# A two-layer graph network: the node block between the layers with its own-part product issued one step ahead and its turn two steps ahead

## The chip, the cores and the metric

The kernel runs on one core of a Trainium2 chip, on real inputs, as one program. The metric is the time of the whole program on the device in microseconds, the median of several runs; lower is better.

## What is computed

The reference applies two graph layers to 6250 nodes of 128 features with 200000 edges `src -> dst`. Ahead of each layer stands a layer norm (no gain, no bias) with a ReLU, and each layer's result is added to its input. Cut to what matters here:

```python
h = relu(layernorm(x))
sums = segment_sum(h[dst], src) + 2 * h;  reduced = sums / (count + 1)
x = x + relu(concat([reduced, h]) @ kernel + bias)            # layer 0
h = relu(layernorm(x))                                        # between the layers
q, k, v = h[src] @ Wq.T + bq, h[dst] @ Wk.T + bk, h[dst] @ Wv.T + bv
att = exp(clip(q.k per head / 4, -10, 10));  out = segment_sum(att / att_sum[src] * v, src)
x = x + layernorm(out + h) * gamma + beta                     # layer 1
```

## The kernel before

The kernel sorts the edges into 49 bins of 128 nodes and then runs layer 0's gathers and segment sums (L526, L1003 to L1005, L767), a **node block between the layers** (L1230 to L1458), layer 1's gathers, attention and sums (L1491 to L1649), and a last node block. The blocks follow one another; within a block each engine has its own program, and semaphores join them.

The block between the layers works in 13 steps of four bins (`NODE_STEPS` = 13, `NT` = 4; the last step has one bin). In step k:

- ScalarE's `first(k)` writes `hs`, the ReLU of the first layer norm (L1393, four instructions), waits for TensorE to have turned it, and copies the turned tiles from PSUM bank 7 to `hT0` (L1399).
- TensorE's `own(k)` turns the four tiles of `hs` (L1358), waits for that copy (`s_e0`), and multiplies: a bias product (L1368) and a product with the lower half of the layer's weights (L1369) for each tile, into bank 6. The reduced half's product is already summed in `acc`.
- VectorE's `update(k)` adds both parts (L1235), adds to `xs` with a ReLU (L1240), and computes the statistics of the second layer norm (L1244 to L1249). ScalarE's `root(k)` takes the root (L1403), VectorE's `scale(k)` makes scale and shift (L1254, L1256), and ScalarE's `normal(k)` writes the second `hs` (L1408).
- TensorE's `turn(k)` turns these tiles (L1340), ScalarE's `copy_h(k)` copies them (L1417), and TensorE's `project(k)` multiplies them with the three weight matrices, 384 columns for each tile (L1349).
- VectorE's `add_bias(k)` writes `qkv` (L1268); SP's queue writes keys and values to DRAM (L1452); ScalarE's `high` (L1421) and `middle` (L1425) and GpSimd's `take_rest` and `take_low` (L1319, L1324) split the queries into three bf16 parts. GpSimd's `plus_beta` (L1314) and `clear` (L1307) prepare layer 1.

The order on every engine is written out by hand: a loop over k calls each stage with a fixed lag. Every engine runs its own instructions in that order. Bank 7 holds one step's turned tiles, bank 6 one step's products, and `hT0` two steps.

Of the kernel before, what the change touches and what calls it, by code (L numbers as in the profile page):

```python
# [82 lines left out]
NODE_STEPS = -(-BINS // NT)  # L83
# [13 lines left out]
def build(nc, x, src, dst, k0, b0, wq, bq, wk, bk, wv, bv, gamma, beta, out):  # L97
# [70 lines left out]
    with ExitStack() as phase:  # L168
# [8 lines left out]
        with nc.Block() as block:  # L177
            c_pool = Count(sem("s_const"))

            @block.sync  # L180
            def _(sp):
                sp.wait_ge(s_pad, 2)
                with nc.allow_non_contiguous_dma("the last edges, one to a partition"):
                    for a, t in ((src, src_i), (dst, dst_e)):
                        sp.dma_start(t[:, 0:FULL], a[0:FULL * P].rearrange("(p c) -> p c", c=FULL))\
                          .then_inc(s_edge, 16)
                        sp.dma_start(t[0:TAIL, FULL:FULL + 1],
                                     a[FULL * P:N_EDGES].rearrange("(p c) -> p c", c=1)).then_inc(s_edge, 16)
                sp.wait_ge(s_xpad, 1)
                head = (BINS - 1) * P  # L190
                sp.dma_start(xs0[:, 0:BINS - 1, :],
                             x[0:head, :].rearrange("(n p) f -> p n f", p=P)).then_inc(s_x, 16)
                sp.dma_start(xs0[0:LAST_NODES, BINS - 1, :], x[head:N_NODES, :]).then_inc(s_x, 16)
# [54 lines left out]
    with ExitStack() as phase:  # L248
# [153 lines left out]
        with nc.Block() as block:  # L402
            @block.sync
            def _(sp):
# [25 lines left out]
                def numbers(row, top):  # L430
                    _, regs = nc.values_load_multi_w_load_instructions(
                        row, engines=[mybir.EngineType.SP], min_val=0, max_val=top,
                        skip_runtime_bounds_check_because="counts of at most N_EDGES edges, beside a bin's start")
                    return regs
# [107 lines left out]
            def _(v):  # L542
# [210 lines left out]
                def add(k, g):  # L753
                    i0 = g * G
                    u = group0[k] + g
                    if i0 % REGS == 0:
                        v.wait_ge(s_rows, k + 1)
                        n = min(REGS, cuts0(k) - i0)
                        _, regs[0] = nc.values_load_multi_w_load_instructions(
                            bin0_row[0:1, k % 2, i0:i0 + n], engines=[mybir.EngineType.DVE], min_val=0,  # L760
                            max_val=BINS - 1, skip_runtime_bounds_check_because="a count of 48 comparisons")
                    v.wait_ge(s_m0, u + 1)
                    for i in range(members(k, g)):
                        if u or i:
                            v.wait_ge(s_a0, added[u] + i)
                        o = acc[:, bass.ds(regs[0][(i0 + i) % REGS], 1), 0:W0].rearrange("p a b -> p (a b)")
                        v.tensor_tensor(out=o, in0=o, in1=bank[5 + u % 3][:, i * W0:(i + 1) * W0], op=ALU.add)\  # L767
                         .then_inc(s_a0, 1)
# [418 lines left out]
    with ExitStack() as phase:  # L1187
# [37 lines left out]
        with nc.Block() as block:  # L1225
# [107 lines left out]
            @block.tensor  # L1333
            def _(t):
                def turn(k):
                    t.wait_ge(s_h1, k + 1)
                    if k >= 2:
                        t.wait_ge(s_e1, k - 1)
                    for i in range(nt(k)):
                        ins = t.transpose(bank[k % 2][:, i * P:(i + 1) * P], hs[:, k * NT + i, :], ident[:, :])  # L1340
                    ins.then_inc(s_t1, 1)

                def project(k):
                    t.wait_ge(s_e1, k + 1)
                    for i in range(nt(k)):
                        n = k * NT + i
                        if n >= 4:
                            t.wait_ge(s_qkv, n - 3)
                        t.matmul(bank[2 + n % 4][:, 0:3 * D], hT1[:, k % 2, i * P:(i + 1) * P],  # L1349
                                 wT[:, :, :].rearrange("p a b -> p (a b)"), start=True, stop=True)\  # L1350
                         .then_inc(s_mm1, 1)

                def own(k):
                    t.wait_ge(s_h0, k + 1)
                    if k:
                        t.wait_ge(s_e0, k)
                    for i in range(nt(k)):
                        ins = t.transpose(bank[7][:, i * P:(i + 1) * P], hs[:, k * NT + i, :], ident[:, :])  # L1358
                    ins.then_inc(s_t0, 1)
                    t.wait_ge(s_e0, k + 1)  # L1360
                    if k:
                        t.wait_ge(s_x1, k)
                    else:
                        t.wait_ge(s_wl2, 16 * 6)
                        t.wait_ge(s_one, 1)
                    for i in range(nt(k)):
                        o = bank[6][:, i * D:(i + 1) * D]
                        t.matmul(o, one_r[:, :], b0_r[:, :], start=True, stop=False)  # L1368
                        ins = t.matmul(o, hT0[:, k % 2, i * P:(i + 1) * P], k0_s[:, 1, :], start=False, stop=True)  # L1369
                    ins.then_inc(s_own, 1)  # L1370

                for i, (a, b) in enumerate(quads):
                    t.wait_ge(s_nat[i], 16 * (b - a))
                    for j in range(a, b):
                        ins = t.transpose(bank[2 + i][:, (j - a) * P:(j - a + 1) * P], nat[:, j, :], ident[:, :])
                    ins.then_inc(s_natT, 1)
                for k in range(NODE_STEPS + 3):
                    if k < NODE_STEPS:
                        own(k)
                    if 0 <= k - 2 < NODE_STEPS:  # L1380
                        turn(k - 2)
                    if k >= 3:
                        project(k - 3)

            @block.scalar
            def _(a):
                def first(k):
                    m = nt(k)
                    for i, (p, q) in enumerate(x_pieces):
                        if k == p:  # L1390
                            a.wait_ge(s_x2[i], 16 if q < NODE_STEPS else 32)
                    for n in range(k * NT, k * NT + m):
                        ins = a.activation(hs[:, n, :], xs[:, n, :], ACT.Relu, scale=rstd[:, n:n + 1],  # L1393
                                           bias=nbias[:, n:n + 1])
                    ins.then_inc(s_h0, 1)
                    a.wait_ge(s_t0, k + 1)
                    if k >= 2:
                        a.wait_ge(s_own, k - 1)
                    a.activation(hT0[:, k % 2, 0:m * P], bank[7][:, 0:m * P], ACT.Copy).then_inc(s_e0, 1)  # L1399

                def root(k):
                    a.wait_ge(s_var1, k + 1)
                    a.activation(rstd[:, cut(k)], rstd[:, cut(k)], ACT.Sqrt).then_inc(s_root1, 1)  # L1403

                def normal(k):
                    a.wait_ge(s_ln1, k + 1)
                    for n in range(k * NT, k * NT + nt(k)):
                        ins = a.activation(hs[:, n, :], xs[:, n, :], ACT.Relu, scale=rstd[:, n:n + 1],  # L1408
                                           bias=nbias[:, n:n + 1])
                    ins.then_inc(s_h1, 1)  # L1410

                def copy_h(k):
                    m = nt(k) * P
                    a.wait_ge(s_t1, k + 1)
                    if k >= 2:
                        a.wait_ge(s_mm1, (k - 1) * NT)
                    a.activation(hT1[:, k % 2, 0:m], bank[k % 2][:, 0:m], ACT.Copy).then_inc(s_e1, 1)  # L1417

                def high(k):
                    a.wait_ge(s_qkv, k * NT + nt(k))  # L1420
                    a.activation(q3[:, cut(k), 0:D], qkv[:, k % 4, 0:nt(k), 0:D], ACT.Copy).then_inc(s_qhi, 1)  # L1421

                def middle(k):
                    a.wait_ge(s_left, k + 1)
                    a.activation(q3[:, cut(k), D:2 * D], left[:, k % 2, 0:nt(k), :], ACT.Copy)\  # L1425
                     .then_inc(s_qmid, 1)

                for k in range(NODE_STEPS + 5):
                    for lag, stage in ((0, first), (1, root), (2, normal), (2, copy_h), (4, high), (5, middle)):
                        if 0 <= k - lag < NODE_STEPS:  # L1430
                            stage(k - lag)

# [342 lines left out]
```

## Time and profile before

| | |
|---|---|
| timed runs, us | 6179.91 median of 3 (6173.57 to 6182.65) |
| profiled execution, us | 6125.97, of which the span of instructions is 6124.2 |
| busy in the whole span, us | TensorE 3137.7, VectorE 3081.1, ScalarE 1860.1, GpSimd 3189.0 |
| mean granted clock of TensorE | 0.614 |
| the block between the layers | 3188 to 3336 us of the span |

The granted clock is given as a share of 2.4 GHz; 0.50 is 1.2 GHz and 1.00 is 2.4 GHz, and a value between them is a stretch in which both occurred. In the rows below PE is TensorE, PEld its weight loads, DVE VectorE, ACT ScalarE, POOL GpSimd. Times are from the start of the span. In order-of-time rows, adjacent instructions of one line are merged ("x4"), and the idle time in brackets is that before the first of them.

### The profile page before, as it was taken

The page shows a single profiled execution, that of the slowest core. Times are in us where ns is not written, and L with a number is a line of the kernel's source. Part 1 is how long each engine was busy: PE and PEld are TensorE (multiplying, and loading weights), DVE is VectorE, ACT ScalarE, POOL GpSimd, SP SyncE. Part 2 cuts the span into 40 slices and gives each one's busy share as a digit, 9 for nine tenths or more (in the row PEclk, how much of TensorE's full clock was granted, in tenths as well). Part 3 has the DMA queues.
Part 4 walks back from the last instruction along what each step waited for, and adds up shares of the span by engine and source line. Part 5 has one row for each costly group of instructions (what it writes and reads, how often), then busy time and mean ns, then how long its engine had stood idle before and what let it go on. Part 6 is the DMA issues. An engine that isn't in the chain of part 4 may idle for free. (4 is left out here: it accounts for less than half of the span.)

```text
span 6124.2 us, 86465 instructions
## 1 busy us (share of the span) xinstructions
PE 3137.7 (51%) x21028; PEld 2407.9 (39%) x21028; DVE 3081.1 (50%) x8514; ACT 1860.1 (30%) x5489; POOL 3189.0 (52%) x3338
## 2 busy tenths in 40 slices
PE   4445445444454354354356555555555555555553
PEld 3223334333233233243234444444444444444442
DVE  6435445455454364354234555555555555555557
ACT  3232433333233333333344222222222222222222
POOL 3363463553543644644634555555555555555554
PEclk8556555556565565565557666666666666666665
DMA  2231231322322322322321222222222222222223
GB/s 78 55 83 47 70 77 49 76 69 51 82 56 56 86 53 60 81 60 64 89 54 63 78 79 79 79 79 79 78 78 79 79 79 79 79 79 79 79 78 58
DMA packets 205061, 436.91 MB, mean 71 GB/s; under 512 B 67172, under 2 KB 114781, under 8 KB 204606
## 3 DMA queue, kind: packets, MB, share of 16 engines
q0 software_dynamic: 153968, 371.50, 23.0%
q1 hardware_dynamic: 49934, 59.56, 3.6%
q8 instruction: 219, 3.59, 0.2%
q14 instruction: 236, 1.93, 0.1%
q10 hardware_dynamic: 704, 0.33, 0.0%
HBM read 415.27 MB, written 55.69 MB: 77 GB/s over the span
## 5 line engine op out<-in xcount | busy, mean ns | idle before, releaser
L526 POOL DMA_INDIRECT got<-hk_table,dst x1563 | 1524.6, 975 | 1487.1 <-PE bank L1005 837.0
L1491 POOL DMA_INDIRECT kv<-kv_table,dst_i x1611 | 1527.1, 948 | 1177.1 <-DVE wv_s L1533 732.5
L767 DVE TENSOR_TENSOR acc<-acc,bank 128x129 f32 x2187 | 634.5, 290 | 1300.2 <-remote 670.8
L1003 PE MATMUL bank<-got,oh 128*128 x2187 | 614.7, 283 | 1294.6 <-DVE acc L767 774.0
L1551 DVE TENSOR_TENSOR acc<-acc,bank 128x136 f32 x1611 | 469.8, 292 | 1232.7 <-remote 822.0
L1003 PEld LDWEIGHTS bank<-got,oh 128*128 128x128 bf16 x2187 | 239.5, 109 | 1495.4 <-issue 1449.3
L1106 ACT ACTIVATE oh<-away 128x384 bf16<-128x384 bf16 x733 | 383.1, 523 | 1392.1 <-remote 803.4
L1622 PE MATMUL bank<-identb,oh 128*128 128x128 bf16 x1611 | 250.1, 286 | 1072.5 <-DVE oh L1504 830.6
L1649 PE MATMUL bank<-wv_s,oh_f 128*128 128x136 f32 x3222 | 782.0, 404 | 3.6 <-DVE wv_s L1533 3.5
L1638 PE MATMUL bank<-q,ohT 128*128 x4833 | 670.4, 276 | 117.4 <-issue 65.1
L1100 ACT ACTIVATE away<-iota,negx 128x128 bf16<-128x128 f32 x2187 | 707.2, 386 | 0.0
L1590 ACT ACTIVATE ohT<-bank 128x384 bf16<-128x384 bf16 x537 | 263.8, 491 | 1444.6 <-remote 1364.8
L1649 PEld LDWEIGHTS bank<-wv_s,oh_f 128*128 128x128 f32 x3222 | 654.4, 287 | 8.9 <-DVE wv_s L1533 4.5
L1005 PE MATMUL bank<-got,oh 128*128 x2187 | 613.1, 282 | 79.9 <-issue 79.6
L1004 PE MATMUL bank<-got,oh 128*128 x2187 | 613.7, 282 | 73.2 <-issue 71.5
L1622 PEld LDWEIGHTS bank<-identb,oh 128*128 128x128 bf16 x1611 | 151.3, 126 | 1167.6 <-DVE oh L1504 883.0
L1638 PEld LDWEIGHTS bank<-q,ohT 128*128 128x128 bf16 x4833 | 496.1, 112 | 283.1 <-issue 193.2
L960 PE MATMUL bank<-oh_t,val 128*128 128x128 f16 x3128 | 350.0, 286 | 73.2 <-issue 48.5
L960 PEld LDWEIGHTS bank<-oh_t,val 128*128 128x128 f16 x3128 | 301.0, 143 | 80.2 <-issue 51.9
L1533 DVE TENSOR_TENSOR wv_s<-kv,bank 128x384 f32<-128x384 f32 x537 | 294.0, 548 | 23.8 <-ACT bank L1601 22.5
L1504 DVE TENSOR_TENSOR oh<-bank,r 128x384 bf16<-128x384 f32 x537 | 295.5, 551 | 7.2 <-ACT bank L1578 7.2
L1512 DVE TENSOR_TENSOR prod<-bank,kv 128x384 f32<-128x384 f32 x537 | 294.4, 548 | 5.8 <-DMA kv<-kv_table,dst_i 3.2
(223 smaller groups left out, 3394.6 us busy)
## 6 DMA issues: line engine op xcount, KB each, us to landing
slots_by_bin<-sorted_chunk SPq DMA_DIRECT2D x637, 61.0 KB
kv<-kv_table,dst_i POOLq DMA_INDIRECT x1611
got<-hk_table,dst POOLq DMA_INDIRECT x1563
kv_table<-qkv SPq DMA_DIRECT2D x12, 512.0 KB, 2.9
hk_table<-hk POOLq DMA_DIRECT2D x6, 772.0 KB, 5.5
out<-o SPq DMA_DIRECT2D x12, 256.0 KB
xs<-in_x SPq DMA_DIRECT2D x3, 768.0 KB, 11.4
sorted_chunk<-vT SPq DMA_DIRECT2D x13, 64.0 KB
```

The source lines that it names most:

```text
L526: g.indirect_dma_start(out=got[:, (tile0[k] + t) % RING0, :], out_offset=None, in_=hk_d, in_offset=bass.IndirectOffsetOnAxis(dst0[:, k % 2 ...
L767: v.tensor_tensor(out=o, in0=o, in1=bank[5 + u % 3][:, i * W0:(i + 1) * W0], op=ALU.add)\
L960: ins = t.matmul(bank[4][:, l * P:(l + 1) * P], val[:, q % 2, l * BLK:(l + 1) * BLK, :, j].rearrange("p w j -> p (w j)"), oh_t[:, q % 2, j ...
L1003: t.matmul(o, w, row(2 * D, 3 * D + 1), start=True, stop=False)
L1004: t.matmul(o[:, 0:D], w, row(D, 2 * D), start=False, stop=False)
L1005: ins = t.matmul(o[:, 0:D], w, row(0, D), start=False, stop=True)
L1100: ins = a.activation(away[:, u % 2, i, :], iota1[:, :], ACT.Abs, scale=1.0, bias=negx[:, k % 2, n:n + 1])
L1491: g.indirect_dma_start(out=kv[:, r, i, :], out_offset=None, in_=kv_d, in_offset=bass.IndirectOffsetOnAxis(dst_i[:, t:t + 1], 0))\
L1551: v.tensor_tensor(out=o, in0=o, in1=bank[4 + u % 2][:, i * W:(i + 1) * W], op=ALU.add)\
L1622: ins = t.transpose(bank[0][:, :].bitcast(BF16)[:, i * P:(i + 1) * P], oh1[:, u % 4, i, :], identb[:, :])
L1638: ins = t.matmul(bank[1 + u % 3][:, i * D:(i + 1) * D], ohT[:, u % 4, i * P:(i + 1) * P], q3[:, bass.ds(regs[0][(s + i) % REGS], 1), j * D ...
L1649: ins = t.matmul(bank[4 + u % 2][:, i * W:(i + 1) * W], oh_f[:, u % 8, i, :], wv_s[:, u % 4, i, :], start=True, stop=True)
```

## The change

On TensorE `own` is split in two. `own_turn(k)` turns the tiles, `own(k)` waits for the copy and multiplies. In the loop, at iteration k, TensorE now issues turn(k-2), own(k+1), project(k-3), own_turn(k+2); it issued own_turn(k), own(k), turn(k-2), project(k-3). On ScalarE `first` moves two iterations ahead, and from the head of the iteration to the place between `copy_h` and `high`. The first steps stand ahead of the loops.

```diff
-                def own(k):
+                def own_turn(k):
                     t.wait_ge(s_h0, k + 1)
                     if k:
                         t.wait_ge(s_e0, k)
                     for i in range(nt(k)):
                         ins = t.transpose(bank[7][:, i * P:(i + 1) * P], hs[:, k * NT + i, :], ident[:, :])
                     ins.then_inc(s_t0, 1)
+
+                def own(k):
                     t.wait_ge(s_e0, k + 1)
...
+                own_turn(0)
+                own(0)
+                own_turn(1)
                 for k in range(NODE_STEPS + 3):
-                    if k < NODE_STEPS:
-                        own(k)
                     if 0 <= k - 2 < NODE_STEPS:
                         turn(k - 2)
+                    if k + 1 < NODE_STEPS:
+                        own(k + 1)
                     if k >= 3:
                         project(k - 3)
+                    if k + 2 < NODE_STEPS:
+                        own_turn(k + 2)
...
+                first(0)
+                first(1)
                 for k in range(NODE_STEPS + 5):
-                    for lag, stage in ((0, first), (1, root), (2, normal), (2, copy_h), (4, high), (5, middle)):
+                    for lag, stage in ((1, root), (2, normal), (2, copy_h), (-2, first), (4, high), (5, middle)):
                         if 0 <= k - lag < NODE_STEPS:
                             stage(k - lag)
```

## Rows read from the trace of the kernel before

**Rows 1.** Busy time by stretch: us, busy us (instructions) of each engine, clock, DMA share, GB/s
```profile
core 0: us, PE busy (x) PEld busy (x) DVE busy (x) ACT busy (x) POOL busy (x), PEclk, DMA share, GB/s
3188.00:3336.00 148.00, 116.24 (x405) 76.64 (x405) 78.46 (x268) 68.72 (x164) 50.57 (x66) 0.74 0.23 68
```

**Rows 2.** Waits inside the block, 3188 to 3336 us: total us, times, longest
```profile
DVE upd L1235 <- PE bank L1369: 48.4, 12, 7.1
...
PEld bank L1368 <- ACT hT L1399: 11.5, 12, 1.1
```

**Rows 3.** TensorE in order of time, one step at the full clock
```profile
3259.06 0.60 PE L1358 MATMUL bank<-ident,hs 128*128 128x128 f32 x4
3260.34 0.48 PE L1368 MATMUL bank<-b_r,one_r 1*128 1x128 f32 x2 [0.69 <-ACT hT L1399]
...
3263.58 0.60 PE L1340 MATMUL bank<-ident,hs 128*128 128x128 f32 x4
3264.01 2.75 PE L1349 MATMUL bank<-wT,hT 128*128 128x384 f32 x8
3267.43 0.66 PE L1358 MATMUL bank<-ident,hs 128*128 128x128 f32 x4 [0.67 <-ACT hs L1393]
```

**Rows 4.** ScalarE in order of time, from three steps
```profile
3265.75 1.63 ACT L1393 ACTIVATE hs<-xs,nbias,rstd 128x128 f32<-128x128 f32 x4
3268.13 0.60 ACT L1399 ACTIVATE hT<-bank 128x512 f32<-128x512 f32 x1 [0.75 <-PE bank L1358]
...
3274.18 0.62 ACT L1421 ACTIVATE q<-qkv 128x512 bf16<-128x512 f32 x1
3274.70 0.62 ACT L1425 ACTIVATE q<-left 128x512 bf16<-128x512 f32 x1
...
3278.96 0.60 ACT L1399 ACTIVATE hT<-bank 128x512 f32<-128x512 f32 x1 [2.11 <-PE bank L1358]
3279.45 0.20 ACT L1403 ACTIVATE rstd<-rstd 128x4 f32<-128x4 f32 x1
3279.55 1.64 ACT L1408 ACTIVATE hs<-xs,nbias,rstd 128x128 f32<-128x128 f32 x4
```

**Rows 5.** Order of time, TensorE and ScalarE at the low clock
```profile
3209.92 1.06 PE L1358 MATMUL bank<-ident,hs 128*128 128x128 f32 x4
3211.02 0.60 ACT L1399 ACTIVATE hT<-bank 128x512 f32<-128x512 f32 x1 [3.10 <-PE bank L1358]
3211.67 0.79 PE L1368 MATMUL bank<-b_r,one_r 1*128 1x128 f32 x2 [0.69 <-ACT hT L1399]
...
3217.32 1.06 PE L1340 MATMUL bank<-ident,hs 128*128 128x128 f32 x4
```

**Rows 6.** Busy time by step, each from its L1358 to the next step's
```profile
3220.60:3232.17 11.57, 10.88 (x32) 7.47 (x33) 4.28 (x21) 4.35 (x11) 1.82 (x3) 0.58 0.01 1
...
3241.40:3249.78 8.38, 7.02 (x33) 4.52 (x32) 5.25 (x21) 5.50 (x13) 2.09 (x4) 1.00 0.18 63
...
3306.74:3336.19 29.45, 14.09 (x42) 7.60 (x40) 11.74 (x29) 11.43 (x28) 17.28 (x20) 0.82 0.22 76
```

**Rows 7.** Busy time and granted clock in a product, and inside two projections
```profile
3222.40:3228.00 5.60, 5.60 (x16) 4.03 (x17) 0.00 (x0) 1.57 (x5) 0.00 (x0) 0.50 0.01 3
3228.90:3230.20 1.30, 1.30 (x4) 0.69 (x4) 1.23 (x4) 1.06 (x3) 0.73 (x3) 0.50 0.00 0
3230.20:3232.00 1.80, 1.80 (x7) 1.13 (x6) 1.73 (x10) 1.07 (x3) 1.09 (x1) 0.97 0.00 0
...
3237.20:3240.60 3.40, 3.40 (x7) 1.87 (x7) 3.26 (x14) 2.65 (x6) 2.52 (x4) 0.51 0.00 0
```

**Rows 8.** TensorE in order of time, the block's last steps
```profile
3310.66 2.75 PE L1349 MATMUL bank<-wT,hT 128*128 128x384 f32 x8
3316.60 1.12 PE L1340 MATMUL bank<-ident,hs 128*128 128x128 f32 x4 [3.20 <-ACT hs L1408]
3317.51 5.20 PE L1349 MATMUL bank<-wT,hT 128*128 128x384 f32 x8
```

## The prediction

> **What bounds the kernel now.** I began with the split of the execution into three stretches [rows 1]. The block that the diff touches lies from 3188 to 3336 us: 148 of 6124.2 us, so nothing in it can be worth more than 2.4%. TensorE is busy for 116.2 us of it, VectorE for 78.5, ScalarE for 68.7 and GpSimd for 50.6, and the clock granted to TensorE is 0.74 on average: a mixture of its two levels, 1.2 GHz (0.50) and 2.4 GHz (1.00). The waits of this stretch [rows 2] show what ends VectorE's idle time, L1369, the product of TensorE's `own`, and TensorE's own wait of 11.5 us in 12 pieces, for ScalarE's copy of the turned tiles (L1399). That is the wait that the change goes for.
>
> Next I read one step in order of time on TensorE, all at the full clock [rows 3], and on ScalarE [rows 4]. TensorE turns (L1358, start 3259.06), waits for the copy, multiplies from 3260.34, turns the normalised tiles (L1340, 3263.58), projects (L1349, 3264.01), and turns again at 3267.43, after a wait of 0.67 us for ScalarE's `hs` (L1393). So the period is a loop through both engines. In numbers: turn to the start of its copy 0.70 (3267.43 to 3268.13), copy to the product 0.65, product 3.24, then from L1340 over ScalarE's copy_h, `high`, `middle` and four ReLUs to the next turn 3.85 (3263.58 to 3267.43). That makes 8.44; the steps that run wholly at 1.00 take 8.38 [rows 6]. At the low clock TensorE alone sets the pace: product 5.65 (3211.67 to 3217.32) [rows 5], a projection about 5.1 (5.20 for the pipelined whole [rows 8]), each turn 0.85. Between the first steady turn, 3220.60, and the last, 3306.74, there are nine periods, mean 9.57 us [rows 6].
>
> **What the change does to this loop.** No instruction is added or removed, and no DMA: SP's queue and GpSimd's keep their order, and their semaphores are the same. Only the order on TensorE and on ScalarE differs. Follow the waits in the new order, at iteration k:
>
> TensorE: turn(k-2), own(k+1), project(k-3), own_turn(k+2).
> ScalarE: root(k-1), normal(k-2), copy_h(k-2), first(k+2), high(k-4), middle(k-5).
>
> `first(k+2)` is two things: four ReLUs, and the copy, which waits for own_turn(k+2). That turn is now the last thing in TensorE's iteration. So ScalarE stands at the copy until TensorE has finished the projection. Queued behind the copy are high, middle, root(k) and normal(k-1), and TensorE's very next instruction, turn(k-1), waits for normal(k-1). The wait for the copy isn't hidden; a longer one takes its place. Before, root and normal ran while TensorE multiplied the `own` part.
>
> The price of the new wait, from own_turn to the next turn: to the copy 0.70; copy to the next instruction 0.50 (3278.96 to 3279.45); high 0.52 (3274.18 to 3274.70), middle 0.52 (the same size); root 0.10 (3279.45 to 3279.55); four ReLUs until TensorE starts on them 1.68 (3265.75 to 3267.43) [rows 3, 4]. Sum 4.02 us, against 1.35 from own_turn to the product before: 2.67 more. What is given back is the wait for `hs`, up to 0.67 in a period at the full clock [rows 3] and nothing at the low one. So a period grows by 2.0 (full clock) to 2.7 us (low clock). After that point nothing else is late: x1(k) and e0(k+1) are ready before own(k+1), since VectorE has 5.3 of 8.4 us of work [rows 6] and now does it inside TensorE's gap; VectorE's last add_bias piece, reciprocal and nbias need about 1.5 us after a projection (the 3.20 us gap in the tail, less the ReLUs' 1.68 [rows 8]), under the 2.34 at which ScalarE comes to normal.
>
> **The clock** is the second term. Read in slices of a microsecond it rose seven times in this block, each time inside a projection; one rise and one fall stand in [rows 7]: one product at the low clock was busy throughout its 5.60 us and the clock stayed at 0.50; the next projection, begun at 3228.9, brought it to 0.97 by 3230.2 [rows 7]. It fell during products, or just after them (0.51 from 3237.2). In the tail a projection ends at full clock, TensorE waits 3.20 us, and the next turn and projection run low from the start (1.12 and 5.20 us, where the projection before took 2.75) [rows 8]. The new order puts a wait of some 3.5 us ahead of every turn and product. I therefore take the product as mostly low: 5.3 (bounds 3.24 and 5.65), and the projection as low for its first part: 4.0 (bounds 2.65 and 5.1; the projection of [rows 7] rose 1.3 us in), the turn 0.6. The steady period is then 4.02 + 0.6 + 5.3 + 4.0 = 13.9, say 14.0 us.
>
> The Trainium skill ("TensorE: Matmul & The Clock Gate", section "HAM oscillation — how this bites in real kernels") says that a wait between bursts of matmuls sends TensorE back to the slow clock and that, in its example, this happened in every tile of the loop. This trace's tail agrees; the middle of a projection speaks against the whole step staying slow. By that page alone every step would be at the low clock, which is the last rival below.
>
> **The sum**, written as start times in the profiled execution. Until own(2) nothing differs: these steps have no turn or projection, and pay the same wait (3209.92 to 3217.32, 7.40 [rows 5]). Then:
> - own_turn(3) at 3217.32 instead of 3220.60; the link to turn(0) without high and middle, low clock (1.10 + 0.50 + 0.10 + 1.68 = 3.38), turn 0.85, product 5.65: own_turn(4) at 3227.2, the same again for own(4) to 3237.1; project(0) 4.2: own_turn(5) at 3241.3. Before, own_turn(5) began at 3241.40, but there a projection and a turn more were already done.
> - own_turn(6): link 2.98 (no high yet) + 0.6 + 5.3 + 4.1 = 13.0, to 3254.3; own_turn(7), with high, 13.5, to 3267.8; five periods of 14.0 to own_turn(12), 3337.8.
> - then link 4.02, turn(9) 0.6, own(12) of one tile 1.1, project(8) 4.1, and a wait for normal(10) like the 3.1 to 3.2 us in the tail of before [rows 8]: turn(10) at 3350.7, project(9) 0.5 later, at 3351.2.
> Before, project(9) began at 3310.66 [rows 8], and from there on both orders are the same. Difference +40.5 us. The profiled execution took 6125.97 us (span 6124.2 and 1.8 around it), 54 us under the median of the timed runs, 6179.91; I add the difference to the median: **6220 us**, +0.65%.
>
> **Rivals.**
> 1. *The clock stays up.* The gap is not long enough to lower it before the product. Product 3.24, projection 2.65, turn 0.43: period 10.34, own_turn(12) at 3312.1, project(9) at 3323.7: +13 us, 6193. With the present mixture of levels, between these and the low figures, about +26, 6206. For it: projections end at 1.00 and several products of before ran at 1.00 after a gap of 0.69. Against it: [rows 8], and products that ran into a fall after only that 0.69. Chance 0.15, both together.
> 2. *The new wait doesn't form and the old one goes.* ScalarE would have to pass high, middle, root and normal before TensorE needs turn(k-1), which is so only if own_turn's result came at least 3.3 us before TensorE's other work ended. Then each of ten periods saves the 1.35 less 0.43 of the turn's own time, 9 us, and the block's waits for `hs` some 4 more: -13 us, 6167, the faster side. For it: ScalarE is idle half of the block [rows 1]. Against it: the order of both queues, read above, leaves nothing between own_turn(k+2) and turn(k-1). Chance 0.04.
> 3. *All low.* The clock never recovers within a projection: period 4.42 + 0.85 + 5.65 + 5.1 = 16.0, project(9) at 3368.4: +58, 6238. For it: the tail's projection of 5.20 us stayed low to its end [rows 8]. Against: the rises inside projections. Chance 0.06.
> 4. *Something hides the new wait in part*, so that the block moves by under 12 us; chance 0.05.
>
> **How the numbers follow.** My case has 0.70. Timed runs of before spread over 9 us, and 0.2% (12.4 us) is about what a measurement can tell from no change. The likeliest time is 6220; the range 6197 to 6238 takes in most of rival 1 and the low-clock bound, and leaves out the faster case and the part-hidden one. Faster: rival 2, 0.03 beyond the bound. Same: the rest of it, rival 4 and a little of rival 1, 0.07. Slower 0.90.
>
> **What would show it.** In the profile after: TensorE's wait for L1399 nearly gone in the steady steps, and L1340 waiting on ScalarE's `hs` (L1408) ten times for about 3.3 us; on ScalarE, the copy L1399 starting right behind each L1358, with the long idle time ahead of it (behind it high and middle, no longer the ReLUs of `first`); a granted clock that is low in most products; a mean period near 14 us in the steady part; a block of about 188 us; nothing moved outside. The prediction is wrong if L1340 does not wait, or if own_turn to turn is under 3 us; only its size is wrong if the periods lie at 10.5 or 16.

## The result and the profile after

The changed kernel is slower: 6233.59 us, median of 4 runs (6218.56 to 6238.76), against 6180.02 for the kernel before (6173.57 to 6182.65). The ratio, estimated from all the runs, is 1.0077, with a 95% interval of 1.0065 to 1.0089: 40 to 55 us (the two medians alone differ by 53.6 us).

The block between the layers now lasts from 3231.5 to 3418.5 us of the span, 187.0 us. Before it was 148.2. (Both are measured from TensorE's first turn of the edge words, L1375 before and L1377 now, to layer 1's first turn.) That is +38.8, where +40.5 was forecast. The whole block in one row, with the columns of [rows 1]:

```profile
3231.50:3418.50 187.00, 134.71 (x406) 87.45 (x407) 84.10 (x269) 67.83 (x165) 52.63 (x66) 0.68 0.18 54
```

TensorE is busy for 18.5 us longer than the 116.2 of [rows 1], with the same matmuls, and idle for the other 20.4 us of the 38.8 (52.3 against 31.9). So in this pair of profiles slower matmuls and more waiting are about equal shares of the loss. (The ends of matmuls are modelled in the profile, so these shares are good to a microsecond or so at best.) Waits inside this block of the changed kernel, by total (us, times, longest):

```profile
ACT hT L1407 <- PE bank L1358: 82.3, 13, 8.8
DVE qkv L1268 <- PE bank L1349: 70.0, 30, 8.0
...
PEld bank L1340 <- ACT hs L1416: 42.2, 13, 3.8
PE bank L1340 <- ACT hs L1416: 37.0, 13, 3.4
DVE upd L1235 <- PE bank L1371: 21.4, 4, 7.2
```

TensorE's wait of 11.5 us for the copy [rows 2] has fallen to that of the first steps, and in front of L1340 TensorE now waits 37.0 us, where it waited 6.5 before. (L1416 is the old L1408, L1407 the old L1399, L1411 the old L1403, L1429 and L1433 the old L1421 and L1425, L1370 and L1371 the old L1368 and L1369; L1358, L1340 and L1349 kept their numbers.) One step of the changed kernel on TensorE in order of time, to be held against [rows 3]:

```profile
3313.87 0.60 PE L1358 MATMUL bank<-ident,hs 128*128 128x128 f32 x4
3317.82 0.66 PE L1340 MATMUL bank<-ident,hs 128*128 128x128 f32 x4 [3.36 <-ACT hs L1416]
3318.41 0.48 PE L1370 MATMUL bank<-b_r,one_r 1*128 1x128 f32 x2
...
3320.47 0.79 PE L1370 MATMUL bank<-b_r,one_r 1*128 1x128 f32 x2
...
3323.22 4.29 PE L1349 MATMUL bank<-wT,hT 128*128 128x384 f32 x8
3327.35 0.60 PE L1358 MATMUL bank<-ident,hs 128*128 128x128 f32 x4
```

and the same step on ScalarE, against [rows 4]:

```profile
3314.51 0.60 ACT L1407 ACTIVATE hT<-bank 128x512 f32<-128x512 f32 x1 [8.02 <-PE bank L1358]
3315.00 0.62 ACT L1429 ACTIVATE q<-qkv 128x512 bf16<-128x512 f32 x1
3315.52 0.62 ACT L1433 ACTIVATE q<-left 128x512 bf16<-128x512 f32 x1
3316.04 0.19 ACT L1411 ACTIVATE rstd<-rstd 128x4 f32<-128x4 f32 x1
3316.13 1.64 ACT L1416 ACTIVATE hs<-xs,nbias,rstd 128x128 f32<-128x128 f32 x4
```

From own_turn's start at 3313.87 to the next turn at 3317.82 are 3.95 us, forecast 4.02. ScalarE idles 8.02 us ahead of the copy, then runs the five pieces in one row while TensorE stands. Inside the product, the pairs of bias matmuls pass from 0.48 to 0.79 us: the clock has fallen. Busy time of that step and of the next, then of the first one's product, projection and link, the stretch from own_turn to the next turn (columns as in [rows 1]):

```profile
3313.87:3327.35 13.48, 10.12 (x33) 6.46 (x32) 6.25 (x21) 5.39 (x13) 4.33 (x5) 0.75 0.12 40
3327.35:3340.88 13.53, 10.18 (x34) 6.54 (x32) 6.26 (x21) 5.39 (x13) 4.33 (x5) 0.75 0.12 39
...
3318.41:3323.22 4.81, 4.81 (x17) 3.46 (x17) 0.41 (x1) 2.13 (x5) 2.13 (x4) 0.61 0.01 3
3323.22:3327.35 4.13, 4.13 (x9) 2.21 (x9) 1.55 (x3) 0.00 (x0) 0.00 (x0) 0.62 0.00 0
3313.87:3317.82 3.95, 0.60 (x5) 0.36 (x3) 3.73 (x16) 3.27 (x8) 1.60 (x2) 1.00 0.39 133
```

The period is 13.5 us in four of the five steady steps and 14.3 in the fifth, 13.7 in the mean (forecast 14.0; 9.57 before). The clock stands at 1.00 in the link, where TensorE works 0.60 of 3.95 us; product and projection get 0.61 and 0.62.

### The profile page after: what moved, and what is told of

It is laid out like the page before. It is cut to its first block and busy times, and to the rows that moved or that the text cites. A ratio compares the mean times of both kernels' runs of the same rounds, so it can differ in the third digit from the quotient of the medians.

```text
span 6232.4 us, 86465 instructions
## 1 busy us (share of the span) xinstructions
PE 3223.9 (52%) x21028; PEld 2473.3 (40%) x21028; DVE 3087.5 (50%) x8514; ACT 1849.6 (30%) x5489; POOL 3173.6 (51%) x3338
## 5 line engine op out<-in xcount | busy, mean ns | idle before, releaser
L1003 PEld LDWEIGHTS bank<-got,oh 128*128 128x128 bf16 x2187 | 239.4, 109 | 1514.7 <-issue 1470.5
L1659 PE MATMUL bank<-wv_s,oh_f 128*128 128x136 f32 x3222 | 832.4, 423 | 8.8 <-issue 4.3
L1659 PEld LDWEIGHTS bank<-wv_s,oh_f 128*128 128x128 f32 x3222 | 695.6, 304 | 8.9 <-DVE wv_s L1543 4.5
L1004 PEld LDWEIGHTS bank<-got,oh 128*128 128x128 bf16 x2187 | 239.8, 110 | 149.4 <-issue 110.7
## 6 DMA issues: line engine op xcount, KB each, us to landing
xs<-in_x SPq DMA_DIRECT2D x3, 768.0 KB, 11.5
```

The source lines that it names most:

```text
L1003: t.matmul(o, w, row(2 * D, 3 * D + 1), start=True, stop=False)
L1004: t.matmul(o[:, 0:D], w, row(D, 2 * D), start=False, stop=False)
L1659: ins = t.matmul(bank[4 + u % 2][:, i * W:(i + 1) * W], oh_f[:, u % 8, i, :], wv_s[:, u % 4, i, :], start=True, stop=True)
```

## Experiments

Times outside the block differed between the chips on which the calls ran: the kernel before took 4559.20 us on the first, 6180.11 on the second, 6113.23 on the third. Each kernel is compared with the kernel before of the same call. "Block" is measured as above, in one profile each; the ratio is estimated from all timed runs of both kernels. Added lines shift the line numbers: what is L1340 in the changed kernel is L1343 in e3, and there L1339 is the added work, L1352 the projection, L1361 the turn ahead of the own product, L1373 and L1374 that product and L1419 the four ReLUs of `normal` (L1414 in e4 and f4).

| run | ratio to before (95%) | block, us | L1340 to L1340, steady steps, us |
|---|---|---|---|
| before, second profile (f2) | | 145.8 | 8.2 to 9.2 |
| changed, second profile (f1) | 1.0068 (1.0051 to 1.0085) | 193.0 | 13.5 to 16.0 |
| e1 splits ahead of first | 1.0080 (1.0063 to 1.0098) | 190.5 | 12.6 to 14.0 |
| e2 turn ahead of project | 1.0085 (1.0068 to 1.0101) | 189.3 | 12.8 to 14.8 |
| e3 filled gap | 1.0051 (1.0039 to 1.0063) | 156.7 (in the fastest of ten, see below) | 10.3 to 12.0 |
| e4 turn right after own | 0.9996 (0.9987 to 1.0006) | 145.2 | 8.9 to 10.5 |
| f3 = e2 + scale first | 1.0001 (0.9992 to 1.0011) | 150.5 | 9.1 to 11.3 |
| f4 = e4 + scale first | 0.9964 (0.9951 to 0.9976) | 128.0 | 6.8 to 8.9 |
| g1 before + scale first | 0.9994 (0.9985 to 1.0003) | 142.6 | 7.9 to 11.3 |
| g2 = e3 with three, + e1 | 1.0051 (1.0036 to 1.0067) | 172.0 | 10.9 to 12.6 |
| g3 = f4 + ReLUs first | 0.9956 (0.9942 to 0.9969) | 120.1 | 6.8 |

**Is it all in the block?** The timed ratio gave 47.6 us, the first pair of profiles 38.8 in the block, and their spans differed by 108. So the changed kernel and the kernel before were profiled again on one chip.

> The changed kernel once more, on the chip of the runs below. The block is 187 us as in its first profile, since the wait and the clock that follow it lie in the kernel's order: about 39 us slower than the kernel before. Rival, that the change costs something outside the block too (the timed difference was 47.6 us by the ratio, the block's only 38.8): the stretches ahead of and behind the block are longer by 5 to 10 us than those of the kernel before in the next run.

> The kernel before once more, one profile, for its stretches on this chip. The block is 148 us; the stretches outside it agree with those of the changed kernel within 5 us.

Busy time by stretch, changed kernel, second profile:

```profile
0.00:3221.00 3221.00, 1485.51 (x10957) 1056.77 (x10957) 1488.61 (x3787) 1085.52 (x3113) 1569.65 (x1636) 0.58 0.26 65
3221.00:3414.00 193.00, 141.93 (x405) 91.53 (x405) 84.33 (x269) 67.77 (x164) 52.48 (x66) 0.65 0.18 52
3414.00:6230.00 2816.00, 1589.18 (x9666) 1311.79 (x9666) 1513.62 (x4459) 697.32 (x2212) 1553.36 (x1637) 0.62 0.28 77
```

and the kernel before, second profile:

```profile
0.00:3218.40 3218.40, 1495.88 (x10957) 1070.85 (x10958) 1489.91 (x3787) 1085.34 (x3113) 1568.84 (x1636) 0.58 0.26 65
3218.40:3364.20 145.80, 112.66 (x405) 74.24 (x405) 79.69 (x269) 68.93 (x164) 50.69 (x66) 0.78 0.25 69
3364.20:6180.40 2816.20, 1595.44 (x9666) 1318.30 (x9666) 1513.58 (x4459) 698.41 (x2212) 1553.27 (x1637) 0.62 0.28 77
```

The stretches outside differ by 2.6 and -0.2 us; the block by 47.2, of a span difference of 49.6. So 47.2 of the 49.6 us lie in the block, and the rival of a cost outside it is out. The first profile of before was an execution with shorter outer stretches (3188.0 and 2788.0). And the block's own time varies between executions: 187.0 and 193.0 for the changed kernel, with a granted clock of 0.68 and 0.65. In this second pair TensorE is busy for 29.3 us longer (141.9 against 112.7) and idle for 17.9 us longer: the added waiting is nearly the 20.4 of the first pair, and the slower matmuls are what varies.

**The link.** Fewer instructions behind the copy.

```diff
-for lag, stage in ((1, root), (2, normal), (2, copy_h), (-2, first), (4, high), (5, middle)):
+for lag, stage in ((1, root), (2, normal), (2, copy_h), (4, high), (5, middle), (-2, first)):
```

> The changed kernel, with high and middle ahead of first on ScalarE, so that only root and normal stand behind the copy. If TensorE waits for the chain behind the copy (my theory), the link from own_turn to turn shrinks from 4.0 to 3.0 us in the seven steps that hold high and middle, L1340 waits about 2.3 instead of 3.35 us, the steady period falls from 13.5 to about 12.5 and the kernel gains 7 to 8 us on the changed one: about 40 slower than before. If the period is set by the clock alone and its rises are tied to times of their own, the period stays near 13.5 and nothing is gained.

TensorE in order of time in e1:

```profile
2403.28 0.60 PE L1358 MATMUL bank<-ident,hs 128*128 128x128 f32 x4
2406.19 1.11 PE L1340 MATMUL bank<-ident,hs 128*128 128x128 f32 x4 [2.32 <-ACT hs L1416]
2412.89 4.37 PE L1349 MATMUL bank<-wT,hT 128*128 128x384 f32 x8
2417.09 0.60 PE L1358 MATMUL bank<-ident,hs 128*128 128x128 f32 x4
```

The link is 2.91 us, as my theory said: 1.04 shorter. But the period is 13.81 and nothing is gained. The turn takes 1.11 and the product runs from about 2407.2 to 2412.89, all low. My expectation of 12.5 was a miss: it took the clock as it was. Over the block TensorE is idle for 6 us less than in the first profile of the changed kernel (46.1 against 52.3) and busy for 10 us more (144.4 against 134.7), so the slower clock took back what the shorter link gave. The rival named there, that the times of the clock's rises set the period, forecast the same result, and this run doesn't rule it out.

**The clock.** Keep the wait and fill the gap with work that nothing reads.

```diff
 def turn(k):
-    t.wait_ge(s_h1, k + 1)
     if k >= 2:
         t.wait_ge(s_e1, k - 1)
+    for i in range(4 if 1 <= k <= 9 else 0):
+        t.matmul(bank[k % 2][:, 0:3 * D], ident[:, :],
+                 wT[:, :, :].rearrange("p a b -> p (a b)"), start=True, stop=True)
+    t.wait_ge(s_h1, k + 1)
```

> The changed kernel, with four extra products of 384 columns put ahead of turn(k), k = 1 to 9, in TensorE's gap; nothing reads them. The wait of the link stays (4.0 us) and TensorE does more work. If the low clock behind the gap is a part of the loss (my theory), products and projections now run at the full clock, the period falls from 13.5 to 10.4 to 11.5 and the kernel gains 15 to 25 us on the changed one. If the clock follows the 128-column products and not the gap, products stay low, the filler takes 4.9 us at the low clock and sticks out of the gap, and the kernel loses 5 to 15 us on the changed one.

Order of time on TensorE in e3, and busy time of that step:

```profile
2398.28 0.60 PE L1361 MATMUL bank<-ident,hs 128*128 128x128 f32 x4
2398.72 2.75 PE L1339 MATMUL bank<-wT,ident 128*128 128x384 f32 x8
2402.24 0.66 PE L1343 MATMUL bank<-ident,hs 128*128 128x128 f32 x4 [0.77 <-ACT hs L1419]
...
2406.06 2.75 PE L1352 MATMUL bank<-wT,hT 128*128 128x384 f32 x8
```

```profile
2398.28:2408.64 10.36, 9.59 (x42) 6.05 (x40) 6.25 (x21) 5.39 (x13) 4.32 (x5) 1.00 0.16 53
```

The busy time of the whole block:

```profile
2306.70:2463.40 156.70, 127.37 (x477) 82.22 (x477) 84.53 (x269) 67.81 (x164) 52.60 (x66) 0.84 0.22 64
```

The link is untouched, 3.96 us from turn to turn (2398.28 to 2402.24), and TensorE does 36 products more. Yet the block falls from 187 to 156.7 us and the clock in it rises from 0.68 to 0.84. The steady period is 10.36, the 10.34 that the prediction gave for "the clock stays up". The added products are busy for 25.8 of the 127.4 us, which leaves 101.6 for the kernel's own matmuls, against 134.7 in the changed kernel and 116.2 in the kernel before. So about 33 us of the changed kernel's matmul time hang on the lowered clock, but some 15 us of such time were in the kernel before as well; the surplus is the 18.5 to 29.3 us read above. At the full clock a steady period is 10.36 us against 8.38 [rows 6]: the wait itself costs 2.0 us a period, what the prediction said.

That profile is not e3's usual execution. It took 4565.49 us, the fastest of ten; one other took 4566.42, and the remaining eight 4577.02 to 4589.50. The median, 4587.79, is 28.6 us above the kernel before, where the profiled execution is 6.3 above. By the medians the filler gains 16 to 25 us on the changed kernel (which lies 45.0 and 53.6 above the kernel before in its two comparisons), as expected, and not the 30 or more of the profiles. The mean clock of the whole span is 0.680 and 0.681 in the two fast executions and 0.674 to 0.679 in the others. That fits a clock that also fell in their blocks, but no trace of one of them was kept, so it isn't shown.

**Both edits**, with three products for the shorter gap.

> The changed kernel with both earlier edits: three extra products of 384 columns in TensorE's gap, and high and middle ahead of first. Each link should now be 1.04 us shorter, and with the clock up that must show in the period: 9.4 instead of the 10.4 us of the filled gap alone, a block of 146 to 150 instead of 156.7 us, the kernel 0 to 6 us slower than before. If the shorter wait gave nothing back in the earlier run for another reason than the clock, the period stays at 10.4.

A miss: the block is 172.0 us and the kernel 31 us slower than before. The link is 2.91 us again (from the turn at 3280.87 to the next at 3283.78), but three products did not hold the clock: none of the seven steps from 3233.76 to 3315.49 has more than 0.85. Two steps of g2:

```profile
3268.32:3280.87 12.55, 12.17 (x40) 7.46 (x39) 5.74 (x21) 5.39 (x13) 4.07 (x5) 0.73 0.12 42
3280.87:3291.88 11.01, 10.63 (x40) 6.51 (x39) 5.52 (x20) 5.39 (x13) 4.08 (x5) 0.85 0.14 48
```

The run doesn't show a shorter link at full clock, so what e1's 1.04 us would be worth there stays untested.

**Hiding the link behind the projection.**

```diff
 if k + 1 < NODE_STEPS:
     own(k + 1)
-if k >= 3:
-    project(k - 3)
 if k + 2 < NODE_STEPS:
     own_turn(k + 2)
+if k >= 3:
+    project(k - 3)
```

> The changed kernel, with own_turn(k+2) ahead of project(k-3) on TensorE, so that the whole link of 4.0 us runs beside the projection of 2.65 to 5.1 us. My theory: L1340 waits 0 to 1 us, the clock is high in more than 0.85 of the block, the period is 7.7 to 9 us, and the kernel is 5 to 12 us faster than before (6168 to 6175). Rival, that issuing own ahead costs by itself (a later update, memory contention): the kernel stays slower than before. Rival, that part of the loss lies outside the block: the block is shorter than before's 148 us but the whole stays about 10 us above before.

A miss: the block is 189.3 us and the kernel 0.85% slower than before. My theory of one loop was too small. Order of time in e2 on three engines:

```profile
2411.43 4.34 PE L1349 MATMUL bank<-wT,hT 128*128 128x384 f32 x8
2411.67 0.60 ACT L1407 ACTIVATE hT<-bank 128x512 f32<-128x512 f32 x1 [3.28 <-PE bank L1358]
...
2415.16 1.20 DVE L1268 TENSOR_TENSOR qkv<-bank,bqkv 128x384 f32<-128x384 f32 x2 [0.38 <-PE bank L1349]
2416.48 0.41 DVE L1256 SCALAR_TENSOR_TENSOR nbias<-mv,rstd 128x4 f32<-128x4 f32 x1
2416.93 1.65 ACT L1416 ACTIVATE hs<-xs,nbias,rstd 128x128 f32<-128x128 f32 x4 [3.53 <-DVE nbias L1256]
...
2418.63 1.12 PE L1340 MATMUL bank<-ident,hs 128*128 128x128 f32 x4 [2.86 <-ACT hs L1416]
```

The copy is early, but VectorE makes nbias only after the add_bias of the projection just done. From the projection's end to the turn are again about 3 us. With scale ahead of add_bias:

```diff
-for lag, stage in ((0, update), (3, add_bias), (1, scale)):
+for lag, stage in ((0, update), (1, scale), (3, add_bias)):
```

> The changed kernel with own_turn(k+2) ahead of project(k-3) on TensorE, and with scale ahead of add_bias on VectorE. The earlier run with the first edit alone still waited 42 us in L1416 for VectorE's nbias, which came after the add_bias of the projection just done. If that was the second, equally long loop (my theory now), it goes: L1340 waits under 1 us, the period is 7.7 to 9, the block 130 to 145 us and the kernel 5 to 18 us faster than before. If the early own part itself costs, the block stays above 180.

The block falls from 189.3 to 150.5: the second loop was real. It is not the 130 to 145 expected, and the kernel is level with before (1.0001) and not faster. A third loop shows. In f3 TensorE's next product waits for VectorE's update, which stands behind add_bias (8.8 us in eight waits); the clock in the block is 0.73, and how much each of the two costs wasn't separated:

```profile
3314.99 1.11 DVE L1235 SCALAR_TENSOR_TENSOR upd<-acc,rc,bank 128x128 f32<-128x128 f32 x4
...
3316.26 0.45 PE L1370 MATMUL bank<-b_r,one_r 1*128 1x128 f32 x2 [1.34 <-DVE upd L1235]
```

**A smaller move.** The own product stays in its step; only the next turn comes early. The diff is against the kernel before, with the guards on k and the first steps ahead of the loops left out.

```diff
 for k in range(NODE_STEPS + 3):
     own(k)
+    own_turn(k + 1)
     turn(k - 2)
     project(k - 3)
...
+for lag, stage in ((1, root), (2, normal), (-1, first), (2, copy_h), (4, high), (5, middle)):
```

> A smaller move: own stays in its own step, and own_turn(k+1) is issued right behind own(k), ahead of turn(k-2) and project(k-3); on ScalarE first(k+1) stands between normal(k-2) and copy_h(k-2). Nothing on TensorE then waits for a copy just asked for. My theory: TensorE-bound, 6.8 us a period at the full clock where ScalarE keeps up (5.4 us of work) or up to 8 where first(k+1)'s ReLUs end after own(k); the block is 10 to 20 us shorter than before's 148, the kernel 6160 to 6172. Rival, that any early own_turn costs elsewhere: no faster than before.

A miss: the block is 145.2 us and the ratio 0.9996, no gain. `normal` waits 31.5 us for nbias. With scale first as well:

> The smaller move (own in its own step, own_turn(k+1) right behind own(k)), with scale ahead of add_bias on VectorE. The first run of the smaller move had L1414 wait 31.5 us for nbias and a period of 9.3. My theory: both waits go, the period is 6.8 to 8 us, the block 125 to 138 and the kernel 10 to 22 us faster than before. If TensorE's clock alone set the period of 9.3, nothing changes: 145.

128.0 us and 0.9964, as expected. The control, scale first in the kernel before:

> The kernel before, with scale ahead of add_bias on VectorE and nothing else. It tells whether the gain of the smaller move (20 us faster with scale first, none without) comes from scale alone. In the kernel before, normal ran beside the own product and had slack, so my theory expects little: the block 140 to 147 us, the kernel 0 to 5 us faster. Rival, that the order on VectorE is the whole gain: 15 to 20 us faster, a block near 128.

142.6 us and 0.9994: the order on VectorE alone is not the gain, and neither is the early turn alone. What scale first does give by itself lies in the block's tail: from the eleventh turn (L1340) to the block's end it is 20.2 us in g1 and 20.1 in f4, against 26.0 before and 26.7 in e4. So of the 17 us between e4 and f4, 6.5 are that tail and 10.6 the steps ahead of it. Last, the four ReLUs at the head of ScalarE's iteration, the copy behind normal:

```diff
-((1, root), (2, normal), (-1, first), (2, copy_h), (4, high), (5, middle))
+((-1, relus), (1, root), (2, normal), (-1, copy_own), (2, copy_h), (4, high), (5, middle))
```

> The smaller move with scale first, and first split in two on ScalarE: the four ReLUs of step k+1 stand at the head of the iteration, the copy after normal. In the run before, own_turn(k+1) still waited up to 1.45 us for these ReLUs, which came after normal. My theory: that wait goes, TensorE is the bound, the period is 7.0 to 8.2 us, the block 118 to 126 and the kernel 24 to 30 us faster than before. Rival: normal, now later, holds turn(k-2) by as much, and the block stays at 128.

TensorE in g3, a step without a wait:

```profile
3242.59 0.60 PE L1358 MATMUL bank<-ident,hs 128*128 128x128 f32 x4
3243.03 0.60 PE L1340 MATMUL bank<-ident,hs 128*128 128x128 f32 x4
3243.47 2.75 PE L1349 MATMUL bank<-wT,hT 128*128 128x384 f32 x8
3246.14 0.48 PE L1370 MATMUL bank<-b_r,one_r 1*128 1x128 f32 x2
...
3249.37 0.60 PE L1358 MATMUL bank<-ident,hs 128*128 128x128 f32 x4
```

The period is 6.78 us (3242.59 to 3249.37), a little under the 7.0 to 8.2 expected, and the block 120.1. The kernel is 27 us faster than before (median 6085.64 against 6113.23), the best version found.

## Why the prediction was right

- **The loop and its price.** Right. L1340 waits 3.35 us in the five steady steps (the prediction: about 3.3, ten times; in the first four it was 2.31 to 2.83, in the tenth 3.03), own_turn to turn is 3.95 us (4.02), and L1358's copy comes 0.64 us after it (0.70). The wait was paid in ten steps and not hidden, so rival 2 is out. At the full clock it adds 2.0 us to a period (8.38 to 10.36 in e3), the 2.0 of the prediction, and TensorE's idle time in the block grew by 20.4 us.
- **The steady period.** 13.7 in the mean of five, not 14.0. Term by term: link 3.95 (4.02), turn 0.7 (0.6), product 5.0 (5.3), projection 4.1 (4.0). The product was the mis-sized term: in four of the five it took 4.6 to 5.0, because the clock stayed up for its first one to two microseconds; in one it was wholly low, 5.65. The early products were wholly low too.
- **The sum.** project(9) starts 161.4 us after the block's beginning (3392.86 less 3231.49), 122.6 before (3310.66 less 3188.02): +38.7 in place of +40.5. Some of that closeness is luck, for errors cancelled: up to own_turn(7) the steps took 2.6 us longer than written down, the five steady ones 1.7 us less, and from own_turn(12) to project(9) it was 10.7 us and not 13.4, since project(8) ran at the full clock (2.75, not 4.1) and the link was shorter. The second pair of profiles gives +47.2 for the block. So in one execution the forecast of the sum is good to some 8 us, no better.
- **The clock.** Right in kind. By the prediction's own figures the order alone gives +26 with the mixture of levels as it was, so some 14 us of its 40.5 are for a clock lower than that. Measured as TensorE's added busy time it was 18.5 us in the first pair and 29.3 in the second: under half of the loss in one, over half in the other. Rival 1 (13 us) is what e3's profiled execution comes to (8.5 to 10.9 us, with the clock at 0.84, above the kernel before's 0.74 to 0.78). Rival 3 (all low, which the prediction also calls the last rival) is out, since every steady projection took 3.9 to 4.5 us and not 5.1. Its one piece of evidence was weaker than said: the tail's projection of 5.20 us did rise just ahead of its end (0.52 over its length).
- **The base.** The difference was added to the median and not to the profiled 6125.97 us, which was right: that execution was short outside the block. The measured median is still 13.6 us above the forecast 6220. The block accounts for 38.8 us in one pair of profiles and 47.2 in the other, the medians for 53.6 and 45.0; that spread isn't explained further.
- **What wasn't seen.** "After that point nothing else is late" held only for this order. Had own_turn been put ahead of the projection, the prediction's method would have promised a gain, as my expectation of e2 did; e2 measured 1.0085, because VectorE's order holds a second loop and, as f3 showed, a third. They were in the order of the stages and in the trace (L1408 waited for nbias already in the kernel before, 10.9 us in nine waits), and I gave that path only a length, not a loop.

## What to carry to other kernels

To issue a producer earlier on one engine helps only if the instruction that waits for it is not followed, in its own engine's order, by something the first engine needs next; write down each engine's order for one iteration and follow the waits round until they close, for every closed loop. Where TensorE's clock moves between its levels, a new gap can cost more than its length: here 18 to 20 us of added waiting came with 18 to 29 us of slower matmuls, and to shorten the gap by a third (e1) gave nothing back. To split a loss of this kind, compare the engine's busy and idle time over the same instructions in both kernels. Check also that the profiled execution is a usual one: e3's was the fastest of ten. Split a stage that both computes and waits, and put the computing half early and the waiting half late.

## What was not expected of the hardware

- The same kernel took 4559 us on one chip and 6113 to 6180 on two others. As far as profiles were taken the difference lies outside this block: in the runs of the first chip layer 0's and layer 1's stretches took about 2307 and 2100 us, in those of the second about 3220 and 2816, while e4's block there (145.2) is close to the kernel before's on the other (145.8). Why the chips differ wasn't tried.
- Extra matmuls in a gap made a block 30 us shorter in the profiled execution of e3, though eight of its ten executions were 12 to 24 us longer than that one. In g2 a step in which TensorE was busy 10.63 of 11.01 us still had a clock of 0.85, where e3's with 9.59 of 10.36 had 1.00. What decides between them stays open.
